# One expert computed densely in token order, and rounds of 8 tiles in place of 16, in a gated cross-attention and mixture-of-experts layer

## What is computed

```python
scores = sigmoid(xf @ w_router)                 # 32 experts
topk_idx = top 6 of (scores + corr_bias), within the best 4 of 8 groups
combine[t, e] = scores[t, e] for the 6 chosen experts, else 0
g = einsum('th,ehm->etm', xf, gate_w)           # H = 256, M = 176
u = einsum('th,ehm->etm', xf, up_w)
eo = einsum('etm,emh->eth', silu(g) * u, down_w)
routed = einsum('te,eth->th', combine, eo)
shared = silu(xf @ sh_gate_w) * (xf @ sh_up_w) @ sh_down_w
x = x + tanh(g_ffn) * (routed + shared)
```

## Time and profile before

| | us |
|---|---|
| median of 3 runs | 283.6 |
| the profiled execution: its time and its span | 284.4 |
| up to the table of tiles (`tiles`, line 1013) | 77.0 |
| first `gate_up` of a tile | 102.3 |
| last `gate_up` pieces | 258 to 261 |
| tiles run | 64 |

### The profile page before, as it was taken

How to read it: one execution, slowest core, us unless ns; L and a number is a source line. 1 busy time by engine, 2 the same in 40 slices (tenths; PEclk the granted TensorE clock), 3 DMA queues, 4 the chain that set the end, 5 groups by cost and what they waited for, 6 DMA issues and landing times.

```text
span 284.4 us, 5136 instructions
## 1 busy us (share of the span) xinstructions
PE 224.2 (79%) x1055; PEld 174.7 (61%) x1056; DVE 126.0 (44%) x521; ACT 86.2 (30%) x237; POOL 159.6 (56%) x146
## 2 busy tenths in 40 slices
PE   7919985976531069999999999999999999999200
PEld 7918774754320037777767777777777777777100
DVE  3478982734901004444334444444444444444325
ACT  3234321000000014443425344444443444443100
POOL 6035675772777702456755766556666556665520
PEclk9765999797995559999999999999999999999755
DMA  5999999899997339999997677666777676544778
GB/s 145 243 218 205 395 404 302 215 346 277 292 352 237 115 104 272 259 296 214 233 237 121 118 135 134 108 109 111 118 118 112 103 115 112 95 54 55 185 198 281
DMA packets 43246, 55.07 MB, mean 194 GB/s; under 512 B 5656, under 2 KB 37752, under 8 KB 43224
## 3 DMA queue, kind: packets, MB, share of 16 engines
q1 hardware_dynamic: 26168, 31.64, 38.9%
q0 software_dynamic: 12432, 19.04, 35.1%
q10 hardware_dynamic: 4624, 4.15, 5.6%
HBM read 32.36 MB, written 22.45 MB: 193 GB/s over the span
## 4 chain that ended last, share of the span: by engine, by line
PE 59%; DVE 14%; issue 9%; DMA 9%; another core or an unknown queue 4%; ACTq 1%; ACT 1%; SPq 0%; POOL 0%; POOLq 0%; DVEq 0%
PE pG L696 27%; PE pY L710 18%; PE pX L690 5%; PE pH L704 5%; DMA sum_dram<-rows,idx 3%; DMA badj<-in_L_xattn_b_dram 3%; PE pY L645 3%; DMA xg<-rows_dram 2%; DMA wgu<-sum_dram 2%; PE pG L634 1%; DVE xs L1071 1%; DVE wgu L925 1%; DVE rows L821 1%; DVE stats L834 1%
## 5 line engine op out<-in xcount | busy, mean ns | idle before, releaser
L696 PE MATMUL pG<-wgu,sdown 128*128 x256 | 88.1, 467 | 16.2 <-issue 16.0
L412 POOL DMA_INDIRECT sum_dram<-xnT,idx x32 | 49.6, 1551 | 41.5 <-ACT xnT L525 32.2
L710 PE MATMUL pY<-wd,sup 88*128 x256 | 65.8, 379 | 0.0
L696 PEld LDWEIGHTS pG<-wgu,sdown 128*128 128x128 f32 x256 | 44.7, 194 | 30.9 <-issue 17.6
L400 POOL DMA_INDIRECT rows_dram<-rows,row_i x48 | 47.4, 987 | 25.5 <-issue 13.5
L1027 DVE COPY sup<-pH 88x256 f32<-88x256 f32 x64 | 26.9, 420 | 67.2 <-PE pH L704 67.2
L710 PEld LDWEIGHTS pY<-wd,sup 88*128 88x128 f32 x256 | 43.5, 190 | 3.7 <-issue 0.2
L412 POOL DMA_INDIRECT sum_dram<-rows,idx x16 | 25.3, 1583 | 17.9 <-ACT rows L525 9.1
L511 ACT ACTIVATE sdown<-pX 128x256 f32<-128x256 f32 x64 | 24.0, 377 | 29.8 <-POOLq L428 28.0
L516 ACT ACTIVATE sgate<-pG 128x176 f32<-128x176 f32 x64 | 20.3, 318 | 33.1 <-PE pG L696 32.4
L704 PEld LDWEIGHTS pH<-ident,sgate 128*88 128x88 f32 x128 | 20.5, 161 | 15.5 <-DVE sgate L1023 0.3
(11 more groups left out here) (166 smaller groups left out, 237.3 us busy)
## 6 DMA issues: line engine op xcount, KB each, us to landing
wd<-in_L_ffn_down_w_dram SPq DMA_DIRECT2D x8, 704.0 KB
wgu<-in_L_ffn_gate_w_dram SPq DMA_DIRECT2D x8, 704.0 KB, 12.9
wgu<-in_L_ffn_up_w_dram SPq DMA_DIRECT2D x8, 704.0 KB, 14.9
sum_dram<-zeros POOLq DMA_DIRECT2D x3, 1152.0 KB
wgu<-sum_dram SPq DMA_DIRECT2D x12, 256.0 KB, 4.5
rows<-rows_dram SPq DMA_DIRECT2D x20, 144.5 KB
xg<-rows_dram ACTq DMA_DIRECT2D x16, 144.5 KB
rows_dram<-zeros SPq DMA_DIRECT2D x8, 289.0 KB, 4.2
```

Of the source, the lines that this page charges most:

```text
L412: pool.indirect_dma_start(sums_dram[INTO[s]][:, :], bass.IndirectOffsetOnAxis(ap=idx[:, s:s + 1], axis=0), y[s], None, compute_op=ALU.add) ...
L696: ins = nc.tensor.matmul(pG[par][:, 0:2 * M].rearrange("t (g m) -> t g m", g=2), xT[:, par, k, :], wgu[:, bass.ds(e, 1), :, k, :].rearrang ...
L710: ins = nc.tensor.matmul(pY[par][:, 0:H], hT[0:MI, par, i, :], wd[:, bass.ds(e, 1), i, :], start=(i == 0), stop=(i == I - 1))
```

## The change

The expert that most of the first 256 tokens chose (the "busy" expert, here 27) is taken out of the table of tiles and computed for all 1024 tokens in token order: its gate and up matmuls read the transposed tokens `xnT` that the router made, so it needs no load, no transpose of tokens, no scaling and no add in DRAM; the VectorE adds its result, times a weight that is zero for tokens that did not choose it, straight into the tokens in SBUF. It stands on the TensorE between `shared_down(3)` and the first tile. SP loads its weights (three transfers of one expert, 528 KB) a second time, ahead of batch 3. The pairs of this expert are still scattered. Rounds are of 8 tiles, so there are 7 rounds; four of them (in place of two) are loaded by the ScalarE. The tile loads before the first tile are all the ScalarE's, put between the busy expert's silus; tiles 5 to 8 are now loaded two in a turn in turns 0 and 1. SP issues all weights in one go, but holds back the last batch until the busy expert's last `down`. The diff, cut to its core (left out: declarations of small tensors and semaphores, and the argument that `add` gets for `INTO_LAST`):

```diff
-ROUND = 16
+ROUND = 8
+HELD = 4
...
-    LEAST = -(-PAIRS // (P * ROUND)) - 1
+    LEAST = -(-(PAIRS - T) // (P * ROUND)) - 1
...
-    FETCH = {t: t - XRING + (t > XRING) for t in range(XRING, 2 * ROUND)}
+    FETCH = {t: max((t - 5) // 2, t - XRING + 1) for t in range(5, HELD * ROUND)}
...
-    AHEAD = 6
-
-
-    INTO = [s % SUMS for s in range(ROUND - 4)] + [0, 1, 0, 1]
-    LEFT = sorted(range(SUMS), key=lambda i: max(s for s in range(ROUND) if INTO[s] == i))
+    PICKED = 3
+
+
+    INTO = [s % SUMS for s in range(ROUND)]
+    INTO_LAST = [2, 0, 1, 2, 0, 1, 0, 1]
+    LEFT = sorted(range(SUMS), key=lambda i: max(s for s in range(ROUND) if INTO_LAST[s] == i))
...
-        xg = [xg_own[:, i, :] for i in range(XRING - JH)] + [rows[:, j, :] for j in range(JH)]
+        xg = [rows[:, j, :] for j in range(JH)] + [xg_own[:, i, :] for i in range(XRING - JH)]
...
-        y = ([xnT[:, k, s * H:(s + 1) * H] for k in range(K) for s in range(T // H)]
-             + [w[:, :, :].rearrange("p j e -> p (j e)")[:, 0:H] for w in (scores, chosen, key, mark)]
-             + [rows[:, j, 0:H] for j in range(JH, J)])
-        ON_ROWS = YRING - (J - JH)
-
+        y = [xnT[:, k, s * H:(s + 1) * H] for k in range(K) for s in range(T // H)]
+
+        busy_gu = xg_own[:, :, :].rearrange("p i c -> p (i c)")[:, 0:2 * K * M].rearrange("p (g k m) -> p g k m", g=2, k=K)
+        busy_d = wd[:, E - BATCH, :, :]
+        not_busy, is_busy, busy_key = (cur[:, i, :] for i in range(SEGS))
...
+                    if i == 7:
+                        sp.wait_ge(s_by, J)
...
-            for i in range(AHEAD):
-                for part in range(3):
-                    weights(i, part)
-
-            sp.wait_ge(s_tiles, 1)
-            sp.wait_ge(s_scat, 16 * JH * TOPK)
-            for t in range(XRING // 2, XRING):
-                load(sp, t, t)
-            for i in range(AHEAD, 8):
+            def weights_of_busy():
+
+                sp.wait_ge(s_busy, 1)
+                e = sp.value_load(busy_i[0:1, 0:1], min_val=0, max_val=E - 1)
+                sp.dma_start(busy_d.rearrange("p i c -> p (i c)"),
+                             down_w[bass.ds(e, 1)].rearrange("e (p i) c -> p (e i c)", i=I)).then_inc(s_busyw, 16)
+                for g, w in enumerate((gate_w, up_w)):
+                    sp.dma_start(busy_gu[:, g, :, :].rearrange("p k m -> p (k m)"),
+                                 w[bass.ds(e, 1)].rearrange("e (p k) m -> p (e k m)", k=K)).then_inc(s_busyw, 16)
+
+            for i in range(8):
+                if i == PICKED:
+                    weights_of_busy()
                 for part in range(3):
                     weights(i, part)
...
-            with sp.Fori(2, ROUNDS) as i:
+            with sp.Fori(HELD, ROUNDS) as i:
...
-            with pool.Fori(1, ROUNDS) as i:
-                with pool.If(i < last + 1):
+            with pool.Fori(1, ROUNDS - 1) as i:
+                with pool.If(i < last):
                     for s in range(ROUND):
                         add(i * ROUND + s, s, i)
+            for s in range(ROUND):
+                add(last * ROUND + s, s, last, INTO_LAST)
...
-                if s >= ON_ROWS and not reused:
-                    act.wait_ge(s_placed, 2)
...
+            def silu_busy(j):
+                act.wait_ge(s_bgu, j + 1)
+                nc.scalar.activation(sg[:, j % 2, :], pG[j % 2][:, 0:M], ACT.Silu).then_inc(s_bsilu, 1)
+
+            silu_busy(0)
             act.wait_ge(s_tiles, 1)
-            act.wait_ge(s_scat, 16 * JH * TOPK)
-            for t in range(XRING // 2):
-                load(act, t, t)
+            for j in range(1, J):
+                silu_busy(j)
+                if j == 1:
+                    act.wait_ge(s_scat, 16 * JH * TOPK)
+                if j <= JH:
+                    load(act, j - 1, j - 1)
             copy_xT(0, 0)
             copy_xT(1, 1)
+            load(act, JH, JH)
             silu(0, 0)
...
-            for i in range(2):
+            for i in range(HELD):
...
+                if b == 0:
+                    for j in js:
+                        ins = nc.tensor.matmul(busy_bank, ones[:, :], chosen_b[:, j, :],
+                                               start=(j == 0), stop=(j == many - 1))
...
-            pe.wait_ge(s_tiles, 1)
...
+            def gate_up_busy(j):
+                for k in range(K):
+                    ins = nc.tensor.matmul(pG[j % 2][:, 0:2 * M].rearrange("t (g m) -> t g m", g=2),
+                                           xnT[:, k, j * P:(j + 1) * P], busy_gu[:, :, k, :],
+                                           start=(k == 0), stop=(k == K - 1))
+                ins.then_inc(s_bgu, 1)
+
+            def turn_h_busy(j):
+                pe.wait_ge(s_bh, j + 1)
+                for i in range(I):
+                    ins = nc.tensor.transpose(pH[j % 2][0:MI, i * P:(i + 1) * P],
+                                              h[:, j % 2, :].rearrange("t (p i) -> t i p", i=I)[:, i, :], ident[:, :])
+                ins.then_inc(s_bhT, 1)
+
+            def down_busy(j):
+                pe.wait_ge(s_bhTc, j + 1)
+                if j < 2:
+                    pe.wait_ge(s_shyc, J - 1 + j)
+                else:
+                    pe.wait_ge(s_byc, j - 1)
+                for i in range(I):
+                    ins = nc.tensor.matmul(pY[j % 2][:, 0:H], hT[0:MI, j % 2, i, :], busy_d[:, i, :],
+                                           start=(i == 0), stop=(i == I - 1))
+                ins.then_inc(s_by, 1)
+
+            pe.wait_ge(s_busyw, 48)
+            gate_up_busy(0)
+            for j in range(J):
+                if j + 1 < J:
+                    gate_up_busy(j + 1)
+                turn_h_busy(j)
+                if j:
+                    down_busy(j - 1)
+            pe.wait_ge(s_tiles, 1)
             transpose_x(0, 1, 0)
             transpose_x(1, 1, 1)
-            pe.wait_ge(s_shyc, J)
+            down_busy(J - 1)
...
+                        if first and t <= 2:
+                            pe.wait_ge(s_byc, J - 2 + t)
...
+                if b == 0:
+                    V.scalar_tensor_tensor(busy_key, busy_bank, 64.0, sign[:, :], op0=ALU.mult, op1=ALU.mult)
...
+            def find_busy():
+
+                link(V.tensor_tensor(busy_key, busy_key, expert[:, :], ALU.add))
+                link(V.max(best[:, J - 1, :], busy_key))
+                V.scalar_tensor_tensor(not_busy, busy_key, best[:, J - 1, 0:1], sign[:, :],
+                                       op0=ALU.not_equal, op1=ALU.mult)
+                link(V.tensor_scalar(is_busy, busy_key, best[:, J - 1, 0:1], None, ALU.is_equal))
+                link(V.tensor_tensor(busy_key, is_busy, expert[:, :], ALU.mult))
+                link(V.reduce_sum(busy_f[:, :], busy_key, axis=X))
+                V.tensor_copy(busy_i[:, :], busy_f[0:1, :]).then_inc(s_busy, 1)
+
+            def weigh_busy():
+
+                link(V.tensor_tensor(chosen[:, :, :], comb, is_busy.unsqueeze(1).to_broadcast([P, J, E]), ALU.mult))
+                link(V.reduce_sum(busy_w[:, :], chosen[:, :, :], axis=X))
...
+            find_busy()
             choose_groups(1)
...
+            weigh_busy()
             shared_gate(9)
             both = count_bank.rearrange("p (a e) -> p a e", a=2)
-            link(V.tensor_tensor(counted[:, :, :], both, sign[:, :].unsqueeze(1).to_broadcast([P, 2, E]), ALU.mult))
+            link(V.tensor_tensor(counted[:, :, :], both, not_busy.unsqueeze(1).to_broadcast([P, 2, E]), ALU.mult))
...
+            def gate_busy(j):
+                dve.wait_ge(s_bsilu, j + 1)
+                V.tensor_tensor(h[:, j % 2, :], sg[:, j % 2, :], pG[j % 2][:, M:2 * M], ALU.mult).then_inc(s_bh, 1)
+
+            def copy_hT_busy(j):
+                dve.wait_ge(s_bhT, j + 1)
+                V.tensor_copy(hT[0:MI, j % 2, :, :].rearrange("p i t -> p (i t)"),
+                              pH[j % 2][0:MI, 0:I * P]).then_inc(s_bhTc, 1)
+
+            def add_busy(j):
+                dve.wait_ge(s_shyc, j + 1)
+                dve.wait_ge(s_by, j + 1)
+                V.scalar_tensor_tensor(xs[:, j, :], pY[j % 2][:, 0:H], busy_w[:, j:j + 1], xs[:, j, :],
+                                       op0=ALU.mult, op1=ALU.add).then_inc(s_byc, 1)
+
+            gate_busy(0)
+            for j in range(J):
+                copy_hT_busy(j)
+                if j + 1 < J:
+                    gate_busy(j + 1)
+                if j:
+                    add_busy(j - 1)
+            add_busy(J - 1)
...
-                    dve.wait_ge(s_shyc, J)
+                    dve.wait_ge(s_byc, J)
```

16 lines of the change are left out of this document (11 added, 5 removed).

## The result

| | before | after |
|---|---|---|
| median of the runs, us | 284.0 (282.77 to 284.5) | 289.32 (287.9 to 290.46) |
| profiled execution: time, span | 284.4, 284.4 | 290.46, 288.6 |
| first `gate_up` of a tile | 102.34 | 118.72 |
| last `gate_up` of a tile | 260.12 | 262.71 |
| from there to the end | 24.3 | 25.9 |

The kernel after is slower: ratio 1.0172, interval 1.0133 to 1.0211. Where the runs of a kernel fall into a faster and a slower group, its ratio rests on the faster one, while a median is that of all its runs. The forecast was 279.5 us, faster, with a range up to 287: both the sign and the range missed. The two spans differ by 4.2 us, and the table says where: the first tile comes 16.4 us later, the 56 tiles take 13.8 us less than the 64 did (not 20.0), and the tail is 1.6 us longer.

What follows compares the result with a forecast made beforehand. PE was taken to bound the kernel at 2.496 us a tile, with a hole from 80 to 102.3 us. Terms -20.0 + 13.6 + 0.75 + 0.5 + 1.0 = -4.1 us gave 280.3 profiled, median 279.5; range 265 to 287.

Steps and rivals of the forecast that it cites:

- eight tiles at 2.496 us: On PE's path: 64 tiles become 56, each worth 2.496 us, so -20.0 us.
- dense part, restart, finding the expert: Before the first tile: six dense blocks left over +13.6 us, restart +0.75, finding and weighing the expert +0.5.
- tile loads on ACT: ScalarE's stream in the first turns: three loads too many at 1.56 us against silu slack; +1.0 us, ends 0 and +3.0.
- last weights: Last three transfers, held for the busy expert's last `down`, take about 12.7 us, needed after 20: 0, 7 us of cover.
- tail: From the last `gate_up` to the end: unchanged, 25 us.
- the crawl of the dense chain: PE in the hole from 80 us: slow work and late signals let two of eight blocks fit; six left, +13.6 us.
- the term for the restart: After the hole: the scatters' aftermath holds the dense chain a little longer; +0.75 us, ends 0 and +1.5.
- the finding of the expert: DVE's `find_busy` and `weigh_busy` plus extra count matmuls, mostly covered by waits: together +0.5 us, ends 0 and +2.8.
- Another sign: Register instructions on ACT between 80 and 103 us should still take 0.7 us.
- The first rival: All eight dense blocks hidden in the hole: -18.0 us, 265.6; chance 0.18 with its half-way cases.
- Rounds and adds: Three more turns of the loops and adds waiting two tiles back: 0, upper end +2 us.
- The second rival: ACT's stream between `silu_busy(0)` and `silu(0)`: nothing hidden, loads late; +3.2 us, 286.8; chance 0.16.

Runs made afterwards that it cites:

- late_rest3: Kernel after, asking for weights per tile, last 24 scatters held back until the dense part is done; chip with late signals: 291.03 us beside 284.75 for the kernel before.
- pre6: Kernel after, asking per tile, buffers of tiles 4 and 5 freed for loads among dense blocks: 0.9888 of before with late signals, 0.9319 without.
- after_defer: Kernel after with the second round unrolled, asking per tile for its expert's weights, buffers unchanged; chip with late signals: 1.0112 of the kernel before.
- again_after: Kernel after, unchanged, measured again on a chip without late signals: 0.9607 of the kernel before.
- own_defer: Kernel after with busy expert's down weights in their own buffer and second round unrolled, asking per tile; chip without late signals: 0.9457 of before.
- again_after2: Kernel after, unchanged, measured once more on a chip with late signals: 1.0184 of the kernel before.

## Why the prediction was wrong, step by step

The sum was -4.1 us and the spans gave +4.2. Term by term, on the first measurement:

| term | predicted | measured |
|---|---|---|
| eight tiles at 2.496 us | -20.0 | -20.0 |
| dense part, restart, finding the expert: first tile | +14.85 | +16.4 |
| first two tiles, at full clock behind the dense part | 0 | -1.7 |
| tile loads on ACT: tiles 3 to 5 | +1.0 | +6.5 |
| last weights | 0 | 0 |
| loops entered (the first) | 0 | +0.05 |
| last round's entry | 0 | +1.35 |
| tail | 0 | +1.6 |
| sum | -4.1 | +4.2 |

*Right: the crawl of the dense chain.* The first tile was to come near 117 us and six of eight `down`s after 102; it came at 118.72, with seven of them after 102. The third `gate_up` was to stand near or after 95; it stood at 87.35, and the fourth at 96.24, so that sign missed by one block. After the last late signal (103.19, 0.85 us later than before, as the term for the restart had it) 15.5 us were left, where six blocks, 13.6, were forecast; the finding of the expert (+0.5) cost nothing, for the second and third group of scatters began at 49.84 and 69.26, before at 50.08 and 69.65. About 2 us of the 15.5 are the lower clock that the first tiles paid before, and here no longer pay: with their -1.7 the first tile's +16.4 is 14.7, against 14.85 forecast. The price came from how PE and its signals behaved in the second group of scatters, and `late_rest3` shows that inference right: without scatters beside it the chain takes 18.8 us on such a chip. Another sign was wrong. Register instructions on ACT were to take 0.7 us again; in the kernel after none of its ten between 80 and 104 us took more than 0.2, and the chain crawled all the same. The signals alone are enough. Slow register work isn't gone, though: in `late_rest3` ACT's take 0.7 us again from 109 us on, beside the moved scatters.

*The first rival's rule describes other chips.* I weighed the Trainium skill (Trainium Architecture — The Big Picture, "What this means for kernel authors": the engines are independent processors), by which the time was 265.6 us. On a chip without late signals the dense part obeys it, with PE busy for 19.00 of 19 us beside the same scatters. (Its times, 260 and 262 us in the two faster runs, aren't to be set against the 265.6, which was worked out from 284.4 for the kernel before.) On a chip with late signals it doesn't: a copy on the VectorE began 8.4 us after PE had done what it waited for. The trace of before showed late signals and I believed it; that there are chips without I couldn't see in it.

*Failed: "Tile loads on ACT ... I take +1.0, ends 0 and +3.0".* The step counted the loads' instructions on the ScalarE and compared them with the silu's slack. The timeline of SP, ACT and PE around the first tiles:

```profile
118.97 0.32 SPq L296 DMA_DIRECT2D wd<-in_L_ffn_down_w_dram  x1
118.98 0.34 ACTq L267 DMA_DIRECT2D xg<-rows_dram  x1
119.39 0.37 SPq L302 DMA_DIRECT2D wgu<-in_L_ffn_gate_w_dram  x1
119.87 0.43 SPq L302 DMA_DIRECT2D wgu<-in_L_ffn_up_w_dram  x1
...
122.44 1.64 ACTq L267 DMA_DIRECT2D xg<-rows_dram  x2
124.13 0.38 ACT L527 ACTIVATE sdown<-pX 128x256 f32<-128x256 f32 x1 [2.30 <-issue]
124.40 0.32 PEld L716 LDWEIGHTS pX<-ident,xg 128*128 128x128 f32 x2 [0.43 <-DMA xg<-rows_dram]
...
130.33 0.51 PE L716 MATMUL pX<-ident,xg 128*128 128x128 f32 x2 [2.46 <-DMA xg<-rows_dram]
```

Tile 3 came 1.0 us late, the very size of the step, but that is luck. The two loads at 122.44 do stand ahead of `copy_xT(3)` at 124.13, yet this was done at 124.52, and `gate_up(3)` began only at 125.34: PE's weight load stood until 124.40 for tile 4's rows, and its sequencer then still had to look up tile 3's expert, until 124.98. What the step left out is the transfer. Tiles 4 and 5 can't be loaded before the eighth dense `gate_up` has read their buffers. Tile 4's load left at 118.98 and tile 5's at 122.44, with 2.1 MB of weights just ahead of them, and tile 5's took 7.84 us where the earlier trace rows has 4.80. And few loaded tiles stood ready to cover it: the kernel before had issued its first eight loads by 104.46, 2.1 us after its first `gate_up`; this one had issued four, and the fifth went out 0.3 us after its own. How much of the 7.84 us the weights made wasn't tested on such a chip. The gaps ahead of tiles 4 and 5 are 6.18 and 4.28 us, +5.5 together; the second is the lower clock that PE fell to over the wait (its four passes from 131.52 took 2.25 us, against 1.19 at 135.96). I had the overlay of the buffers before me and asked neither when the transfer could leave nor how many tiles cover it. `pre6` sends these two loads earlier (and no longer two in a turn) and gains 2.2 points on `after_defer` on the same chip.

*Failed: "Rounds and adds ... 0".* The two boundaries read in the earlier trace rows are entries of passes that are run. The code allows for 10 rounds (ROUNDS) and 7 run, so PE's sequencer also goes through three skipped passes ahead of the last round; in the kernel before it went through one, and no gap showed. +1.35 us, inside the upper end of +2.

*Right by luck of the chip: the weights, "0, with 7 us of cover".* On a chip without late signals tiles start 30 us sooner, and the same wait after 8 tiles costs 8.7 us in the profiled execution of `again_after`. Even so the gain is 4% there; `own_defer`, without that wait and with the buffer of its own, gains 5.4%.

*Tail: unresolved.* It was 25.9 us against 24.3, two adds landing in 6.06 and 6.08 us. But the tail of the other kernels lies anywhere between 23.9 (`own_defer`) and 26.0 (`pre6`), and that of `again_after2`, the same kernel, was 24.6. So I don't put it down to the change.

The second rival (nothing hidden and loads late, 286.8 us) was nearest in its sum and half right in its mechanism: the loads were late, but by their transfers and not by crowding, and two blocks were hidden.

## What to carry to other kernels

When a change takes a preload away, ask of each remaining load when its buffer is free, what is in the queues then, and how many items of work stand ready to cover it; instruction time on the issuing engine is the small part. When it makes a round shorter or starts the loop earlier, look for every "wait for all" that is placed by rounds: it moves with them. And a hole that is made by late signals fills slowly with work that itself passes signals between engines several times a step: here two blocks of eight went into it. Long stretches on one engine should do better, which no run here tried.

## What the runs showed of the hardware

The same kernel takes different times on different chips: the kernel before 284 to 286 us on three and 270 to 274 on four others, each measured at one time only; and the change gained 4% on one and lost 1.8% on another. In the first kind PE's signals reach ACT and DVE up to 10.5 us late in a copy (104.99 for transposes done at 94.45, `again_after2`) and 12.9 us late in a silu (102.46 for a `gate_up` done at 89.60, the kernel after) while POOL issues indirect scatters 1.28 us apart; the last late one came 3.1 to 4.6 us after the last scatter of a burst had started (64.24 and 67.29, 98.60 and 103.19, 100.95 and 104.99 us). With the scatters held back the same chain ran at PE's pace. A skipped pass of a runtime loop costs PE's sequencer 0.75 us. In one run 2.53 us of idling ended at the lower clock, which cost a further 2.5 us.
